# State sums of a selective scan on TensorE: one 128x128 diagonal product per item, or four 64x64 quarters per pair of items

## The reference

```python
xz = x @ in_proj_w.T + in_proj_b
x_in, z = jnp.split(xz, 2, axis=-1)                  # 512 channels each
x_conv = jax.nn.silu(conv4(x_in))                    # causal, 4 taps
dt_low, Bm, Cm = x_conv @ x_proj_w.T                 # 64, 16, 16 columns
dt = jax.nn.softplus(dt_low @ dt_proj_w.T + dt_proj_b)
A = -jnp.exp(A_log).T                                # 16 states per channel
def step(h, inp):                                    # over 2048 positions
    A_bar = jnp.exp(dtt[..., None] * A)
    B_bar = (A_bar - 1.0) / safe_A * Bt[:, None, :]
    h = A_bar * h + B_bar * xt[..., None]
    y = jnp.einsum('bds,bs->bd', h, Ct) + D * xt
    return (h, y)
y = ys * jax.nn.silu(z)
return y @ out_proj_w.T + out_proj_b
```

## Time and profile before

| | |
|---|---|
| time, median of 3 runs | 2742.09 us (2737.33 to 2742.41) |
| span of the profiled execution | 2716.5 us |
| its own time | not listed apart from the runs; the span lies 25.6 us under the median |
| busy, share of the span | PE 93%, DVE 84%, POOL 84%, ACT 67%, weight loads 53% |
| mean granted TensorE clock | 0.975 |
| the largest group on PE | the sums over states, L1040, 857.6 us with `dg_inv` and 217.4 us with the identity |

### The profile page before, as it was taken

The page is one execution under the profiler, slowest core; times in us unless marked ns, Lnnn a source line. Parts: engine busy times, 40 slices in busy tenths (PEclk is TensorE's granted clock), DMA queues, the critical chain, the costliest instruction groups (busy, mean ns, idle before and its releaser), DMA issues. The chain is left out here.

```text
span 2716.5 us, 37230 instructions
## 1 busy us (share of the span) xinstructions
PE 2518.4 (93%) x9666; PEld 1447.6 (53%) x9666; DVE 2283.9 (84%) x3740; ACT 1832.6 (67%) x3655; POOL 2286.1 (84%) x2127
## 2 busy tenths in 40 slices
PE   6899999999999999999999999999999988799997
PEld 3445555555545455545555555455554544488874
DVE  3898989898989898889898998989898989755546
ACT  5576767777686767676868676777767675355537
POOL 2899898989898989899898989898989898666654
PEclk8999999999999999999999999999999989899999
DMA  3233343434333434343334334343333334478667
GB/s 89 96 112 113 107 129 103 130 101 125 111 118 108 119 106 121 113 120 115 113 119 116 111 111 127 105 130 101 125 110 117 112 106 138 156 218 249 206 202 245
DMA packets 249004, 349.65 MB, mean 129 GB/s; under 512 B 75863, under 2 KB 123611, under 8 KB 248412
## 3 DMA queue, kind: packets, MB, share of 16 engines
q1 hardware_dynamic: 233196, 302.47, 37.3%
q0 software_dynamic: 15600, 44.79, 4.7%
HBM read 288.72 MB, written 58.45 MB: 128 GB/s over the span
## 5 line engine op out<-in xcount | busy, mean ns | idle before, releaser
L685 POOL TENSOR_TENSOR hc<-h,c_rep 128x512 f32<-128x512 f32 x832 | 1048.2, 1271 | 99.8 <-DMA c_rep<-bc_rows 47.4
L1040 PE MATMUL y_ps<-hc,dg_inv 128*128 128x512 f32 x1664 | 857.6, 607 | 17.6 <-POOL hc L685 15.4
L668 POOL TENSOR_TENSOR h<-x_conv,b_rep 128x512 f32<-128x512 f32 x640 | 803.9, 1269 | 35.3 <-PE y_ps L1040 14.1
L1233 DVE TENSOR_TENSOR_SCAN h<-a_ps,carry,h 128x512 f32<-128x512 f32 x640 | 807.6, 1270 | 9.7 <-ACT score L836 5.4
L778 ACT ACTIVATE a_ps<-dt,a_mat 128x512 f32<-128x512 f32 x640 | 438.6, 687 | 411.4 <-DVE h L1233 408.0
L1062 PEld LDWEIGHTS g_ps<-b_steps,x_conv_rows 128*128 128x128 f32 x3072 | 404.2, 194 | 232.4 <-issue 200.4
L1217 DVE SCALAR_TENSOR_TENSOR h<-a_ps,h 128x512 f32<-128x512 f32 x640 | 428.3, 669 | 92.4 <-ACT a_ps L778 92.3
L1040 PEld LDWEIGHTS y_ps<-hc,dg_inv 128*128 128x128 f32 x1664 | 286.8, 191 | 305.2 <-issue 226.5
L1062 PE MATMUL g_ps<-b_steps,x_conv_rows 128*128 128x128 f32 x3072 | 413.5, 278 | 30.4 <-ACT x_conv_rows L861 16.9
L778 ACT ACTIVATE h<-dt,a_mat 128x512 f32<-128x512 f32 x384 | 268.9, 712 | 60.8 <-POOL hc L685 60.5
L1241 DVE TENSOR_TENSOR_SCAN h<-g_ps,carry,h 128x512 f32<-128x512 f32 x192 | 245.4, 1278 | 24.0 <-ACT h L778 20.6
(11 more groups left out here) (269 smaller groups left out, 3479.6 us busy)
## 6 DMA issues: line engine op xcount, KB each, us to landing
c_rep<-bc_rows SPq DMA_DIRECT2D x512, 256.0 KB, 3.4
b_rep<-bc_rows SPq DMA_DIRECT2D x320, 256.0 KB, 3.7
gathered<-slot_rows SPq DMA_DIRECT2D x144, 129.5 KB, 3.5
gathered<-y_planes SPq DMA_DIRECT2D x32, 512.0 KB, 7.7
x_t<-in_x_t SPq DMA_DIRECT2D x16, 512.0 KB, 4.5
x_tok<-in_x_tok SPq DMA_DIRECT2D x16, 512.0 KB, 4.1
out<-x_t SPq DMA_DIRECT2D x16, 512.0 KB, 3.1
x_t_rows<-y_gated SPq DMA_DIRECT2D x15, 512.0 KB, 2.6
```

Source lines behind the costliest of these rows:

```text
L668: nc.gpsimd.tensor_tensor(h[:, i % SLOTS, e], x_conv[:, u[1] % 2, chunk(i, e)], b_rep[:, n % BS], ALU.mult).then_inc(u_ready, 1)
L685: nc.gpsimd.tensor_tensor(hc[:, i % HCS, e], h[:, i % SLOTS, e], c_rep[:, i % CS], ALU.mult).then_inc(hc_pool, 1)
L1040: nc.tensor.matmul(y_ps[:, e], by, hc[:, i % HCS, e], start=first_one, stop=(i % HALF == HALF - 1)).then_inc(summed, 1)
L1233: nc.vector.tensor_tensor_scan(slot, a_ps[:, e], slot, before_it, ALU.mult, ALU.add).then_inc(scanned, 1)
```

## The change

The sum over states is no longer one 128x128 product per item. A diagonal matrix is zero outside its two 64x64 diagonal blocks, so each item is made of two products of 64 rows by 64 columns: channels 0 to 63 from the partitions 0 to 63, channels 64 to 127 from the partitions 64 to 127. The four products of a pair use the four 64x64 quarters of the array: item 0 takes (rows low, columns low) and (rows high, columns high), item 1 (low, high) and (high, low). What comes from the low partitions is written to bank 0 of `y_ps`, what comes from the high ones to bank 1. So each bank now holds halves of both chunks: bank 0 has the low half of chunk 0 and of chunk 1, bank 1 the high half of chunk 1 and of chunk 0 ("mixed"). The gate must have its channels in the same order, so the host lays out the z rows of the input projection and its bias, and the rows of the output projection, in this order (`by_halves`); that costs nothing on the chip.

`add_pair` stands at the odd slot and waits for both hc of its pair; `add_item` stood at both slots. The skip term is now added by PE, with the identity and by the same quarters, at slots 33 and 47 (`add_skip`), so `make_gated` loses its addition on DVE; and GATED_AT moves by one slot, to 35, 36, 3 and 4, each of the two now waiting for the whole half.

```diff
+QUARTER = P // 2
+        SKIP_ADD_AT = (33, 47)
-            def add_item(u, i, e):
+            def add_quarters(by, v, e, start, stop):
+                low, high = slice(0, QUARTER), slice(QUARTER, P)
+                nc.tensor.matmul(y_ps[QUARTER * e:QUARTER * (e + 1), 0], by[low, low], v[low], start=start, stop=stop)
+                return nc.tensor.matmul(y_ps[QUARTER * (1 - e):QUARTER * (2 - e), 1], by[high, high], v[high], start=start, stop=stop)
+            def add_pair(u, i):
                 p, first_one = i // HALF, i % HALF == 0
                 if first_one:
-                    wait(pe, gated, count(u, CH, 2 * (p - 1) + e + 1))
-                hc_wait(pe, u, i, e)
+                    wait(pe, gated, count(u, CH, 2 * p))
                 s = state(i)
-                by = dg_inv[:, chunk(i, e), pool_slot(s)] if on_pool(i) else ident[:]
-                nc.tensor.matmul(y_ps[:, e], by, hc[:, i % HCS, e], start=first_one,
-                                 stop=(i % HALF == HALF - 1)).then_inc(summed, 1)
+                hc_wait(pe, u, i, 0)
+                hc_wait(pe, u, i, 1)
+                for e in range(2):
+                    by = dg_inv[:, chunk(i, e), pool_slot(s)] if on_pool(i) else ident
+                    add_quarters(by, hc[:, i % HCS, e], e, first_one, i % HALF == HALF - 1).then_inc(summed, 1)
+            def add_skip(u, p):
+                pe.wait_ge(skip_ready, count(u, CH, 2 * p + 2))
+                for e in range(2):
+                    add_quarters(ident, skip[:, e], e, False, False).then_inc(skip_added, 1)
...
             def make_gated(u, c):
-                dve.wait_ge(summed, count(u, ITEMS, (c // 2 + 1) * ITEMS // 2 - 1 + c % 2))
-                dve.wait_ge(skip_ready, count(u, CH, c + 1))
-                nc.vector.tensor_tensor(y_ps[:, c % 2], y_ps[:, c % 2], skip[:, c % 2], ALU.add).then_inc(skip_added, 1)
+                dve.wait_ge(summed, count(u, ITEMS, (c // 2 + 1) * ITEMS // 2))
                 dve.wait_ge(gate_ready, count(u, 1, c // 2 + 1))
-                dve.wait_ge(skip_added, count(u, CH, c + 1))
...
-            GATED_AT = {ITEMS // 2 + 2 * LAG - 2: 0, ITEMS // 2 + 2 * LAG - 1: 1, 2 * LAG - 2: 2, 2 * LAG - 1: 3}
+            GATED_AT = {ITEMS // 2 + 2 * LAG - 1: 0, ITEMS // 2 + 2 * LAG: 1, 2 * LAG - 1: 2, 2 * LAG: 3}
...
+    def by_halves(v):
+        v = v.reshape((CH // 2, 4, QUARTER) + v.shape[1:])
+        return v[:, [0, 2, 3, 1]].reshape((DI,) + v.shape[3:])
```

More of the change, by code:

```diff
@@ L1155, in unit_program @@
                     pu, pi = before(u, i, LAG)
-                    if not (plan is second and i < LAG):
-                        add_item(pu, pi, e)
+                    if e == 1 and not (plan is second and i < LAG):
+                        add_pair(pu, pi)
+                    if m in SKIP_ADD_AT:
+                        add_skip(u, SKIP_ADD_AT.index(m))
                     for at, ni, ne in DU_PLACE:
@@ L1175, in _ @@
             for i in range(PAIRS - LAG, PAIRS):
-                for e in range(2):
-                    add_item((0, UNITS - 1), i, e)
+                add_pair((0, UNITS - 1), i)
         @block.vector
@@ L1440, in stack @@
         return np.concatenate([g[f"L0_ffn_experts_{name}"], g[f"L0_ffn_shared_{name}"][None]])
+    def by_halves(v):
+        v = v.reshape((CH // 2, 4, QUARTER) + v.shape[1:])
+        return v[:, [0, 2, 3, 1]].reshape((DI,) + v.shape[3:])
+    in_proj, in_bias = g["L0_attn_in_proj_w"], g["L0_attn_in_proj_b"]
     up = np.concatenate([stack("wg"), stack("wu")], axis=2)
     return {
+        "w_in": chunks(np.concatenate([in_proj[:DI], by_halves(in_proj[DI:])]).T),
+        "b_in": chunks(np.concatenate([in_bias[:DI], by_halves(in_bias[DI:])])),
+        "w_out": chunks(by_halves(g["L0_attn_out_proj_w"].T)),
         "w_gate": chunks(g["L0_ffn_gate_w"]),
```

## The result

The changed kernel takes 2802.46 us (median of 4 runs, 2795.22 to 2811.82) beside 2739.71 us of before: a ratio of 1.0235, 95% interval 1.0208 to 1.0262. The forecast was 2700 us, faster. It is 63 us slower. Of two kernels further down, filled at slot 44 and at slot 44 and three more places, one execution in twelve took 7563 and 3808 us; these two are not in the ratios.

A forecast was written before the change was run, and what follows sets the result against it. PE, at 135.2 of 143.4 us a unit, was taken as the bound, POOL (130.2) and DVE (129.4) close behind. About 4 us gained less 1.5 gave 2.5 a unit, 40 for 16: 2742 - 40, about 2700 us; range 2665 to 3090.

The forecast's parts named there:

- the quarters run side by side: PE's sums: all four quarters of a group work together, 49.9 us a unit against 55.0, PE wins 5.1; chance 0.45.
- stagger: PE's groups: the last quarter starts behind six weight loads of 0.055 us, 0.33 us late; 10.2 us a unit over 31 runs.
- Rival A: PE's queue: a quarter's second matmul blocks the next quarter; 27 us a unit more on PE, 3070 us; chance 0.27.
- B: PE's groups: row halves run independently, columns overlap one step; +1 us a unit, 2758 us; chance 0.18.
- C: PE's groups: only low and high run together, some 2950 us, or nothing does, some 3800; chance 0.05.
- a trip into another size and back: PE's tile-size switches: 0.39 us each, 27 more trips a unit, 10.5 us a unit.
- DVE's 126.7: DVE's busy time per unit, from 129.4 us, after four additions of 0.679 us go.
- All other pairs lose little: add_pair waits for the second hc, but POOL makes it anyway before it needs the buffer back.: Pair sums away from the turns of the halves: summing both items at the odd slot was given no cost.
- the turn of the halves: PE's first group of a half, slot 37, waits for both gatings; 1.5 us a unit on POOL, bounds 0 and 4.
- the clock was left at nothing: PE's granted clock, 0.99 before: more gaps might bring the lower level more often, adding to any case; no size given.
- "Half of PE's 5.1 and a part of DVE's 2.7" is paid back: Unit time: shrinking waits return about 4 us a unit, 2.5 after the 1.5 at the turns of the halves.
- rival D: Whole kernel: PE gets lighter and nobody uses it, POOL's 130.2 us and waits set the pace; 2735 to 2745; chance 0.05.

The follow-up runs named there:

- filled at slot 44: Changed kernel with four hc buffers and both gatings at slot 35 (and 3), plus two zero products on PE before slot 44's g_ps products: 0.9974 of before.
- slot 44 and three more places: The kernel filled at slot 44, plus four zero products before each of PE's long waits at slots 0, 22 and 55: 0.999 of before.
- four buffers: Changed kernel with four hc buffers instead of two, the skip term sharing the memory of `square`: 1.0102 of before, unit 145.17 us.
- the gatings at slot 35 and two buffers: Changed kernel with both gatings behind the scan of slot 35 (and 3), still two hc buffers: 1.0179 of before, unit 144.95 us.
- ring and gate mended: Changed kernel with four hc buffers and both gatings behind the scan of slot 35 (and 3): 1.0028 of before, unit 143.65 us.

## Why the prediction was wrong

**Right: the quarters run side by side,** the case that I held likeliest. My term for it was 0.86 us and 0.33 of stagger. The stagger does not exist: the weight loads of the quarters overlap like their matmuls, here at another group,

```profile
1152.06 0.13 PEld L1037 LDWEIGHTS y_ps<-hc,dg_inv 64*64 64x64 f32 x1 [0.76 <-POOL hc L687]
...
1152.08 0.13 PEld L1038 LDWEIGHTS y_ps<-hc,dg_inv 64*64 64x64 f32 x1
```

where I had put them 0.055 us apart. The span of one matmul plus a few ns for each further tile (the Trainium skill, "TensorE: Matmul & The Clock Gate", Part 3) holds here with two passes on each tile: the first passes start within 0.02 us. Rival A, for which the rule of strict program order spoke, falls, and B and C with it; whether the second passes stand directly behind the first in PE's queue, as A had it, the trace does not tell. My 0.39 us for a trip into another size and back was too much too: 0.09 before the group, 0.11 behind its second passes and 0.11 in the products after it, 0.31. Both errors were on the careful side: PE gained 13.5 us a unit of queue time or more, not 5.1, near the 15.3 that I had worked out without the stagger. DVE's 126.7 came out as 127.3.

**Wrong, the first step that failed: "All other pairs lose little: add_pair waits for the second hc, but POOL makes it anyway before it needs the buffer back."** With two buffers, POOL's hc of item 0 two pairs on needs what the sum of both items frees. One slot later was too late 107 times in thirteen units: 11.6 us a unit of waiting on POOL, whose 130.2 us of work I had named as the limit. Most of that wait replaced others; what the ring costs the kernel is what four buffers take off, 1.3 to 1.5%, some 2 us a unit. I had the rule at hand (the wait for `summed` of the pair two before) and did not lay the slots of the two engines side by side.

**About right: the turn of the halves.** I named the mechanism, PE's queue with DVE's g_ps products behind the late gating, and priced it at 1.5 us a unit, 0 to 4. In the change it is worth 1.0 us a unit by the ratios (1.0235 to 1.0179) and with four buffers 1.3 (1.0102 to 1.0028); the units of the profiled executions differ by more, 2.3 and 1.5, but one of these executions was the fastest of four. The delay itself is 22.3 us in 25 waits of PE or 0.9 each, where I had said 1. In the kernel before, with its fuller PE, the same step measures 3.9.

**Wrong, the second step that failed: the clock was left at nothing.** I wrote that a lighter PE given the lower level "would add to any case" and put no number to it. The half level covers 14% of the units (266 of 1914 us) instead of under 3% (48 of 1864). The part that counts lies near slot 44, where DVE waits behind it. Mean unit against undisturbed units gives its price, an estimate: 2.3 of the 3.85 us that the unit of the changed kernel lost, from 147.26 and 145.0; 1.8 with four buffers, from 145.17 and 143.4; 1.6 with the gatings at slot 35 and two buffers, from 144.95 and 143.4. It is as large as the ring's, and the two are not independent. The filling of slot 44 showed 0.5% of it, once the other two were mended.

**"Half of PE's 5.1 and a part of DVE's 2.7" is paid back: hardly.** With ring and gate mended the unit is 143.65 us with a PE that has 11 us less to do. That is the outcome of rival D, to which I gave 0.05: the gain of a lighter PE went into PE's own waits. It is not the whole of it: in the two kernels filled at slot 44 and at all four places, the units in which no wait of DVE for g_ps is lengthened behind the half level take 141.6 to 142.3 us, about 1.2 less than the usual 143.1 of before, where I had taken 4; in the other units the lower level takes this back. The rows that should have warned me were there: PE's waits in the earlier trace rows are for DVE and ACT, and DVE's largest wait is for ScalarE's decays, not for PE. What sets the pace among DVE, ACT and POOL was not tested.

The range of 2665 to 3090 held the time by luck, only because it reached to rival A, whose mechanism did not happen.

## What to carry to other kernels

An edit that merges two steps of one engine moves when buffers come free: list for each ring the slot at which its owner needs it and the slot at which it is freed, before and after, because a one-slot move in an in-order program cost 2.2% here, and a primitive that took 1.22 us in place of 1.72 gave nothing. When an engine is made lighter, the time shows only where someone waits for it; look at which instructions stand behind its waits, and at the granted clock there. Compare the repetitions of one loop within one trace: where the same instructions took 144.9 us once and 150.6 another time, the clock was what differed, and a mean over all of them hides it. If a wait of TensorE is followed by products that another engine waits for, work in that wait can be worth more than none.

## What the runs showed of the hardware

- Four 64x64 quarters of float32, two MATMUL each, start within 0.02 us, second passes 0.48 us later; the next full-size product starts 1.02 us after the first, and with what the neighbours lose the group costs 1.22 us where two full-size items cost 1.72.
- The half level fell on TensorE's work behind a wait of 1.88 us, and with two products of zeros in the wait the granted clock stayed at 1.00. Four such products before each of three other waits raised the clock of the units from 0.94 to 0.96.
- The same list of instructions with the same wait of 1.53 us ran at a granted clock of 1.00 in one unit and 0.67 in another, over 20 us. Eight g_ps products took 1.06 us to the next row in the one and 1.97 in the other.
- The time outside the units depends on the chip. From the last gate to the end it is 372 to 375 us in every profile of the sets where before took 2719.93 and 2720.06 us, and 388 to 394 in the sets where it took 2735 to 2740, whatever the kernel. The profile of before has 374.7, that of the changed kernel 394.9, so some 20 of the 78 us between their spans are not the change's. Spans of different sets are not to be compared, only ratios and units.
